# Eight products on constants in each round of a threshold search, on TensorE

## The reference

```python
probs = jax.nn.softmax(h @ r2_w.T, -1)
topp, topi = jax.lax.top_k(probs, TOPK)
...
routed = hit.any(1)
...
score = jnp.where(routed, probs, -jnp.inf)
idx = jnp.argsort(-score, axis=0)[:cap].T
```

## Time and profile before

| | us |
|---|---|
| median of three runs (lowest, highest) | 1682.98 (1675.51, 1683.24) |
| the profiled execution's own time | 1683.95 |
| its span, first to last instruction | 1682.2 |
| TensorE busy | 1427.2 |
| VectorE busy | 1071.8 |
| ScalarE busy | 906.7 |
| GpSimd busy | 423.8 |
| mean granted TensorE clock | 0.912 |

### The profile page before, as it was taken

The page is one execution under the profiler, slowest core; times in us unless marked ns, Lnnn a source line. Parts: engine busy times, 40 slices in busy tenths (PEclk is TensorE's granted clock), DMA queues, the critical chain, the costliest instruction groups (busy, mean ns, idle before and its releaser), DMA issues. The chain is left out here.

```text
span 1682.2 us, 34515 instructions
## 1 busy us (share of the span) xinstructions
PE 1427.2 (85%) x12381; PEld 1152.4 (69%) x12381; DVE 1071.8 (64%) x2945; ACT 906.7 (54%) x1594; POOL 423.8 (25%) x370
## 2 busy tenths in 40 slices
PE   2399999999999999999999553325999999999996
PEld 1266676767767666677666452325989999999996
DVE  3246655555656656566665358796777777777773
ACT  0177666666757667676666113433445555555552
POOL 0011212111212212122111000002445555555553
PEclk8699999999999999999999555558999999999998
DMA  3532433333343424334210323002556655655652
GB/s 119 137 92 78 125 96 92 99 89 103 85 105 83 125 66 122 87 101 123 71 54 33 122 80 3 0 0 71 173 137 183 181 149 169 184 167 152 183 154 24
DMA packets 128692, 177.38 MB, mean 105 GB/s; under 512 B 19966, under 2 KB 116996, under 8 KB 124484
## 3 DMA queue, kind: packets, MB, share of 16 engines
q1 hardware_dynamic: 111172, 154.49, 31.1%
q0 software_dynamic: 17408, 21.25, 7.7%
HBM read 134.28 MB, written 41.41 MB: 104 GB/s over the span
## 5 line engine op out<-in xcount | busy, mean ns | idle before, releaser
L612 ACT ACTIVATE at<-ps_s 128x1024 f32<-128x1024 f32 x256 | 248.7, 1027 | 42.0 <-PE ps_s L499 39.5
L195 PE MATMUL ps_s<-xet,whi 128*128 128x322 f32 x640 | 206.9, 323 | 17.9 <-issue 11.0
L1760 POOL DMA_INDIRECT out_rows<-ye,slot_token x96 | 151.1, 1574 | 230.1 <-ACT ye L1618 218.4
L196 PE MATMUL ps_s<-xet,wlo 128*128 128x322 f32 x640 | 201.1, 314 | 0.0
L197 PE MATMUL ps_s<-xet,whi 128*128 128x322 f32 x640 | 199.7, 312 | 0.0
L1587 ACT ACTIVATE sg<-ps_s 128x322 f32<-128x322 f32 x160 | 70.5, 440 | 170.8 <-PE ps_s L197 155.2
L1682 DVE TENSOR_TENSOR wlo<-raw,whi 128x640 fp32r<-128x640 f32 x192 | 156.9, 817 | 1.3 <-ACT whi L1597 1.3
L499 PE MATMUL ps_s<-q,k 32*128 32x256 f32 x2048 | 151.1, 410 | 0.0
L195 PEld LDWEIGHTS ps_s<-xet,whi 128*128 128x128 f32 x640 | 122.3, 191 | 26.0 <-issue 26.0
L195 PE MATMUL ps_av<-whi,hs 128*128 128x256 f32 (+1 forms) x480 | 135.2, 282 | 2.9 <-DVE wlo L1682 2.9
L516 PE MATMUL ps_av<-at,uv 128*16 128x257 f32 x2048 | 135.9, 383 | 0.0
(11 more groups left out here) (352 smaller groups left out, 3508.3 us busy)
## 6 DMA issues: line engine op xcount, KB each, us to landing
raw<-in_wexp SPq DMA_DIRECT2D x32, 1280.0 KB, 6.3
halo<-gray_dram SPq DMA_DIRECT2D x96, 288.0 KB
xb<-in_x SPq DMA_DIRECT2D x64, 384.0 KB, 4.7
raw<-in_wexp SPq DMA_DIRECT2D x32, 640.0 KB
gray_dram<-g SPq DMA_DIRECT2D x32, 256.0 KB, 3.2
out_rows<-h SPq DMA_DIRECT2D x64, 128.0 KB, 6.3
token_rows<-xf SPq DMA_DIRECT2D x64, 128.0 KB, 3.5
pre_dram<-pre SPq DMA_DIRECT2D x32, 128.0 KB, 5.1
```

The source lines that it names most:

```text
L195: nc.tensor.matmul(o, lh, rh, start=first, stop=False)
L196: nc.tensor.matmul(o, ll, rh, start=False, stop=False)
L612: nc.scalar.activation(at[:, t, 2 * i:2 * i + 2, :, 0:R].rearrange("p j k q -> p (j k) q"), ps_s[i][:, :, :, :].rearrange("p j k q -> p (j ...
L1760: nc.gpsimd.indirect_dma_start(out=out, out_offset=bass.IndirectOffsetOnAxis(ap=slot_token[0:w, 3 * m + st:3 * m + st + 1], axis=0), in_=y ...
```

## The change

After the product of constants and before the wait for the counts, TensorE does eight more products in each round but the last: `same_e` times `same_e`, 128x128 by 128 columns in float32r, all to the same 128 columns of a bank of `ps_s[0]`, each overwriting the one before. Nothing reads them.

```diff
                 pe.wait_ge(cand_set, b + 1)
                 if b < BITS - 1:
                     nc.tensor.matmul(tot, cst[:, CBE:CBE + 128], shift2[:, :], start=True, stop=False)
+
+                    for _ in range(8):
+                        nc.tensor.matmul(ps_s[0][:, 0, 0, 0:128], same_e[:, :], same_e[:, :], start=True, stop=True)
                     pe.wait_ge(signs, b + 1)
                 pe.wait_ge(counted, b + 1)
                 nc.tensor.matmul(tot, same_e[:, :], tally2[:, :], start=b == BITS - 1, stop=True).then_inc(totals, 1)
```

## The result

The changed kernel takes 1701.78 us, median of four runs (1697.18 to 1706.06); the kernel before takes 1682.07 us, median of four (1675.51 to 1683.24). The ratio is 1.0118, 95% interval 1.0094 to 1.0142: slower by 1.2%, clear of the noise. The profiled execution took 1706.06 us with a span of 1703.7, against 1683.95 and 1682.2 before.

The account below looks back on a forecast made before the run. The prediction took each search round's chain of count, product and two VectorE operations as the bound; 28 rounds of 0.73 us delay at half clock add 20.4 us, giving 1703.4 us, range 1696 to 1711.

Parts of the forecast that it names:

- The bound: Search rounds: count, product, two small VectorE operations form the chain; TensorE is on it only from +1.43 to +1.80 us.
- The price of a product: New TensorE products in the search: 0.214 us from one to the next at half clock.
- The sum: Search: tallies' load starts at +2.16 instead of +1.43, each round 0.73 us longer, 28 rounds, 20.4 us.
- The clock: Search: full clock lost after the first round, half clock in all later rounds.
- the first rival: Search at full clock in most rounds: nothing late, 0.11 us gained a round, 3.1 us in all; chance 0.08.
- Full clock all through: Search: products all in by +1.20, 28 rounds each gain 0.11 us, 3.1 us, total 1680; chance 0.08.
- The tail: Few products following the search: up to 1.5 us more gained if the full clock holds into them.
- Hidden at half clock: Search: products 0.107 us apart, eight in 0.86 us, no change, 1683 us; chance 0.07.
- the break-even pitch of 0.122 us: Search at half clock: the spacing from which eight products would be hidden, (1.43 - 0.45) / 8.
- To and fro: Search: clock changes, half of the rounds at full clock, 8.7 us longer, 1692 us; chance 0.10.
- No overlap at all: Search: each new product costs its whole 0.41 us, a round 2.3 us more, 64 us, 1747; chance 0.05.
- The total: Whole kernel: 20.4 us on the profiled 1683.95 gives 1704.4; 1703.4 against the median of three runs.

Follow-up runs that it names:

- e2_sixteen: Changed kernel with sixteen new products a round instead of eight, same place: round 4.80 us, search 139.79 us.
- e4_narrow: Changed kernel with the eight products on 32 moving columns instead of 128: round 3.09 us, search 90.38 us.
- e7_bf16: Changed kernel with the eight products in bfloat16 instead of float32r: round 2.37 us, search 70.66 us.
- e8_behind: Changed kernel with the eight products moved behind the product with the tallies: round 2.37 us, search 70.21 us.
- e10: Changed kernel with twelve products of 256 columns behind the tallies' product, instead of eight of 128 ahead: round 2.26 us, search 68.32 us.
- e12: Twelve products of 256 columns behind the tallies' product, timed over 12 runs: 1681.92 us, ratio 0.9999 to the kernel before; search 68.79 us.
- e11_split: Changed kernel with eight products of 256 columns ahead and four more behind the tallies' product: 1678.03 us, ratio 0.9993 to the kernel before; search 69.02 us.
- e9_behind256: Changed kernel with eight products of 256 columns behind the tallies' product, instead of 128 ahead: round 2.26 or 2.37 us, search 68.44 us.
- e3_wide: Changed kernel with the eight products on 256 moving columns instead of 128, same place: round 3.09 us, search 90.29 us.
- e5_dense256: Changed kernel with eight products of 256 columns, router weights as operands instead of mostly zeros: round 3.09 us, search 91.37 us.

## Why the prediction was right

**The bound.** A round is count, product, two small operations of VectorE, and TensorE is on it only at its end. Right: L1268's load came 0.67 us later and the next count 0.72, and no other stage moved by more than it does from one execution to the next.

**The price of a product.** 0.214 us, from five rows of the same form in another stage; measured 0.214 (e2_sixteen against the changed kernel). I had the size from a row and left open what it was made of. It is not the moving columns (e4_narrow) and it goes with the type (e7_bf16), which leaves the load or a fixed price of four-byte products; the narrow loads of L1284 speak for the load.

**The sum.** I put L1268's load at +2.16 and it came at +2.10, because L1262's two passes take 0.39 us from their first load to the first new one (1038.14 to 1038.53), not two full pitches of 0.43: the new loads start at +0.40, not at +0.45. The comparison then follows 0.53 us after that load's start, 0.04 more than where the load comes alone: behind other products the tallies' product starts 0.11 us after its load (1040.23 and 1040.34), and 0.03 after it where it stands alone. Together 0.67 + 0.04 = 0.71; from count to count a round is 0.72 us longer, not 0.73. 28 x 0.72 = 20.2, and the first round, which I thought free, lost 0.12: its clock fell half-way. Together 20.3 us against the forecast 20.4; measured in the search 20.28. The two errors (0.73 for 0.72 in 28 rounds, nothing for 0.12 in the first) are small and cancel in part.

**The clock.** Right that it stays at half. The stretch from 979.1 to 982.5, busy without a gap at 0.50, was the good argument, and e8_behind shows the like of it in the search. I had the full clock lost after the first round; it fell within it, 0.8 us after the first count in the changed kernel's profiled execution and 1.8 us in the kernel before's, so the later rounds had it to win back, and did not. The Trainium skill's advice to keep TensorE busy ("TensorE: Matmul & The Clock Gate", section "Why this matters for your kernels") fits e10 to e12, but not e8_behind, whose TensorE is busy 99% of the time at 0.50. So the condition that I gave the first rival ("as soon as the clock is granted in most rounds") can be met, but not by products of 128 columns, at least not by four, eight or sixteen ahead or eight behind, and not by eight of 256 ahead.

**The rivals.** Full clock all through: not in this kernel; where it was brought about (e11_split) it gave what I had priced, products ahead of the wait hidden and 2.26 us a round. The tail that I had priced at up to 1.5 us gave 0.1: in e10, e11 and e12 the stretch from the last count to the first gather takes 52.06 to 52.08 us for 52.17. Hidden at half clock: the break-even pitch of 0.122 us fits, bfloat16 gets below it and is hidden, float32r does not and is not. The Trainium skill's 0.107 us ("TensorE: Matmul & The Clock Gate", section "Back-to-back issue gap") fits e7's bfloat16 products (about 0.10) and is half of what float32r shows (0.214). The same section gives that figure for the product by itself and says that in a stream the loads set the spacing too, which my prediction left out; by it the skill doesn't speak for this rival as plainly as I wrote. To and fro: seen in e9_behind256 alone. No overlap at all: out, in every run.

**The total.** Forecast 1703.4, measured 1701.78, against a median of before that was 0.9 lower than the one that I had; the medians lie 19.7 us apart. That the totals agree so closely is in part luck, since four runs of the changed kernel spread over 9 us. What bears out the sum is the search, read to 0.01 us.

## What to carry to other kernels

Filler on an engine that stands idle is free only up to the moment at which the work behind it in program order is released: find that moment in the timeline, divide the gap by the pitch of the filler (start to start) from rows at the clock that is granted, and put the filler behind the critical instruction, not ahead of its wait. Don't take full rows of TensorE for the full clock: eight products of 128 columns behind the critical one kept it busy 99% of the time at 0.50, and twelve of 256 in the same place had 1.00 from the fourth round on. And ask first what the full clock is worth: here 0.11 us a round, against 0.72 us for the attempt.

## What the runs showed of the hardware that I had not expected

- A granted clock of 0.50 with TensorE busy 59.53 of 60 us and its loads 59.24 (e8_behind): the busy rows don't tell the clock.
- At half clock a float32r product of 256 columns costs as much as one of 32: eight of them make a round of 3.09 us in both (e3_wide and e4_narrow).
- In e9_behind256 the same work that brought 1.00 left TensorE idle for 2.47 of 6.70 us once it ran at 1.00, and the clock fell, again and again; e10, with half as many products more, stayed at 1.00. That the idle time is the cause of the fall is not shown.
- Operands of 97% zeros and operands of normal numbers gave the same clock and the same pitch (e3_wide and e5_dense256).
